# Loading the message stage's rows into two alternating sets of six buffers

## The chip, the cores and the metric

The kernel runs on one core of one Trainium2 chip. The metric is the device time of one execution in microseconds (us). A profiled execution gives the rows that are read below.

## The reference

Two graph layers run on 6250 nodes with 64 features and 206250 edges, the self loops among them, sorted by their destination. The change lies in the last step of the first layer, where each edge's message (64 features in each of 4 heads, 256 numbers) is weighted by the edge's attention and added up over the edges of a destination:

```python
alpha = segment_softmax(alpha, i, N_NODES)
msg = out_j * alpha[:, :, None]
aggr = jax.ops.segment_sum(msg, i, num_segments=N_NODES)
out = aggr.mean(1) + bias
```

`out_j` (one row of 256 numbers for an edge) was computed by earlier stages and lies in DRAM, in the two tensors `rows0` and `rows1`. A row there has 324 numbers, of which the message stage reads the first 256. The second layer is a graph convolution (`gcn_conv` twice), with a layer norm behind each layer.

## The kernel before

The kernel is a sequence of stages, each with its own tiles, and with a barrier of all engines between two of them. Only `message_stage` is touched. It goes through 152 iterations of 6 units (`BU = 6`); a unit is 256 rows, as 128 partitions by `UT = 2`. The 152 iterations are two parts of 75 and 77 (`z.its`). `paired_parts` emits each part as pairs of iterations: the first pair straight, the pairs between as a loop whose body holds two iterations, then the last pair and one single iteration straight. Of the 37 pairs of the first part 35 are in its loop, and 36 of the second part's 38, so that 142 iterations run inside the loops and 10 are straight code.

For unit j of iteration i the engines do this:

- **SP** (`load`) waits until the rows of iteration i-1 in buffer `oj[j]` are used (`oj_used[j]`) and issues the DMA `oj[j]<-rows` of 256 KB at L2330. Its queue is in order: what waits for unit 3 holds back units 4 and 5.
- **POOL** (`weigh`) first copies the iteration's attention into `heads` (L2340) and then makes the weighted message `msg[j]` (L2346) for the units of `WEIGHED`, 0, 1, 2, 4 and 5. Each waits for its DMA (`oj_in[j]`) and until TensorE has read the message of iteration i-1 (`summed[j]`).
- **DVE** makes the second one-hot matrix `onem` (L2386) of units 0, 2 and 4, weighs unit 3 itself (L2391), and adds each unit's sum from PSUM into `acc` (L2400). In front of each unit it reads the unit's block number into a register (`value_load`). Its order within an iteration is: onem of unit 2, add 0, message 3, add 1, onem 4, add 2, add 3, onem of the next iteration's unit 0, add 4, add 5.
- **ACT** makes the other one-hot matrices (L2358, L2368) and copies the attention beside the message (L2371).
- **PE** sums: two products of `onem` and `msg` into `psm[j]` (L2425), which the trace shows as 4 matmuls for a unit. It waits for `onem`, the message and the attention of its unit, in the order of the units.

The lines that set these waits are:

```python
wait(eng, oj_used[j], i)                                   # SP, before the load of unit j
eng.wait_ge(oj_in[j], (i + 1) * 16)                        # POOL, and DVE for unit 3
wait(eng, summed[j], i)                                    # POOL, before it writes msg[j]
eng.wait_ge(oj_used[j], i + 1)                             # PE, the message is there
```

The tiles and semaphores are made per unit number: 6 `oj`, 6 `msg`, 6 PSUM banks.

Of the kernel before, what the change touches and what calls it, by code (L numbers as in the profile page):

```python
# [15 lines left out]
fp32 = mybir.dt.float32  # L16
# [6 lines left out]
P = 128  # L23
D = 64
H = 4
C = H * D
K = 8
UT = 2
BU = 6
# [71 lines left out]
def wait(eng, semaphore, value):  # L101

    if not isinstance(value, int) or value > 0:
        eng.wait_ge(semaphore, value)


def rounds(eng, n, emit, start=0):

    if n - start > 0:
        emit(start)  # L110
    if n - start > 2:
        with eng.Fori(start + 1, n - 1) as i:
            emit(i)
    if n - start > 1:
        emit(n - 1)
# [12 lines left out]
def paired_parts(eng, counts, emit):  # L128

    first = 0  # L130
    for h, n in enumerate(counts):
        def two(i, first=first, h=h):
            emit(first + 2 * i, h)
            emit(first + 2 * i + 1, h)

        rounds(eng, n // 2, two)
        emit(first + n - 1, h)
        first += n


# [5 lines left out]
def seg(i, j, depth):  # L146

    return (i + 1, j - depth) if j >= depth else (i, j)
# [2146 lines left out]
def message_stage(nc, z, m, sb, ps, sem):  # L2295

    n_it = z.NU // BU
    with ExitStack() as ctx:
        oj = [sb(ctx, f"oj{j}", [P, UT, H, D], fp32) for j in range(BU)]
        ND = BU  # L2300
        msg = [sb(ctx, f"msg{q}", [P, UT, C + H], fp32) for q in range(ND)]
        one = [sb(ctx, f"onem{q}", [P, UT, P], fp32) for q in range(ND)]
        psm = [ps(ctx, f"psm{q}", [P, 512], fp32) for q in range(BU)]
        dist = [sb(ctx, f"dist_m{q}", [P, UT, P], fp32) for q in range(ND)]
        heads = sb(ctx, "heads", [P, H, BU * UT], fp32)
        heads_kept = sem(ctx, "heads_kept")
        WEIGHED, BOTH = (0, 1, 2, 4, 5), (1, 3, 5)
        second_ready = [sem(ctx, f"onem_second{j}") for j in range(BU)]
        dist_ready = sem(ctx, "distm_ready")
        placing = sem(ctx, "placing")  # L2310
        one_ready = [sem(ctx, f"onem_ready{j}") for j in range(BU)]
        oj_in, oj_used, weights_ready, summed, added = ([sem(ctx, f"{s}{j}") for j in range(BU)] for s in (
            "oj_in", "oj_used", "weights_ready", "msg_summed", "msg_added"))
        block = ctx.enter_context(nc.Block())
        rows = [r.rearrange("(u p k) c -> u p k c", p=P, k=UT) for r in m["rows"]]

        def tiles(i, j, h):

            h = int(i >= z.its[0]) if isinstance(i, int) else h
            return rows[h][span((i - h * z.its[0]) * BU + j, 1)].rearrange("o p k c -> (o p) k c")  # L2320

        def last(i):
            return isinstance(i, int) and i == n_it - 1

        @block.sync
        def _(eng):
            def load(i, h):
                for j in range(BU):
                    wait(eng, oj_used[j], i)
                    eng.dma_start(oj[j][:, :, :, :].rearrange("p k h d -> p k (h d)"),  # L2330
                                  tiles(i, j, h)[:, :, 0:C]).then_inc(oj_in[j], 16)

            paired_parts(eng, z.its, load)

        @block.gpsimd
        def _(eng):
            def weigh(i, h):
                wait(eng, oj_used[WEIGHED[-1]], i)
                eng.sem_inc(placing, 1)
                eng.tensor_copy(heads[:, :, :], m["alpha"][:, :, span(i * BU * UT, BU * UT)]).then_inc(heads_kept, 1)  # L2340
                eng.wait_ge(heads_kept, i + 1)
                for j in WEIGHED:
                    eng.wait_ge(oj_in[j], (i + 1) * 16)
                    wait(eng, summed[j], i)
                    eng.sem_inc(placing, 1)
                    eng.tensor_tensor(msg[j][:, :, 0:C].rearrange("p k (h d) -> p k h d", h=H), oj[j][:, :, :, :],  # L2346
                                      heads[:, :, j * UT:(j + 1) * UT].rearrange("p h t -> p t h")[:, :, :, None]
                                      .to_broadcast([P, UT, H, D]), ALU.mult).then_inc(oj_used[j], 1)

            paired_parts(eng, z.its, weigh)  # L2350

        @block.scalar
        def _(eng):
            def away(i, j):
                o, c = before(i, j, ND, BU)
                wait(eng, summed[o], c)
                for k in range(UT if j in BOTH else 1):
                    ins = eng.activation(dist[j % ND][:, k, :], m["io128"][:, :], ACT.Abs,  # L2358
                                         bias=m["nloA"][:, span((i * BU + j) * UT + k, 1)])
                ins.then_inc(dist_ready, 1)  # L2360

            def body(i, h):
                for j in range(BU):
                    if not (last(i) and j + 1 >= BU):
                        away(*seg(i, j + 1, BU))
                    eng.wait_ge(dist_ready, i * BU + j + 1)
                    n = UT if j in BOTH else 1
                    eng.activation(one[j % ND][:, 0:n, :], dist[j % ND][:, 0:n, :], ACT.Relu, bias=1.0,  # L2368
                                   scale=-1.0).then_inc(one_ready[j], 1)

                    eng.copy(msg[j % ND][:, :, C:C + H],  # L2371
                             m["alpha"][:, :, span((i * BU + j) * UT, UT)].rearrange("p h t -> p t h"))\
                       .then_inc(weights_ready[j], 1)

            away(0, 0)
            paired_parts(eng, z.its, body)

        @block.vector
        def _(eng):
            def product(i, j):  # L2380
                q = j % ND
                o, c = before(i, j, ND, BU)
                t = (i * BU + j) * UT
                wait(eng, summed[o], c)
                if j not in BOTH:
                    eng.tensor_scalar(one[q][:, 1, :], m["io128b"][:, :], m["nloA"][:, span(t + 1, 1)], 0.0, ALU.add,  # L2386
                                      ALU.is_equal).then_inc(second_ready[j], 1)
                if j in WEIGHED:
                    return
                eng.wait_ge(oj_in[j], (i + 1) * 16)  # L2390
                eng.tensor_tensor(msg[q][:, :, 0:C].rearrange("p k (h d) -> p k h d", h=H), oj[j][:, :, :, :],  # L2391
                                  m["alpha"][:, :, span(t, UT)].rearrange("p h t -> p t h")[:, :, :, None].to_broadcast([P, UT, H, D]),
                                  ALU.mult).then_inc(oj_used[j], 1)

            def add(i, j, b):
                eng.wait_ge(summed[j], i + 1)
                o, c = before(i, j, 1, BU)
                wait(eng, added[o], c)
                a = m["acc"][:, bass.ds(b, 1), :].rearrange("p o c -> p (o c)")
                eng.tensor_tensor(a, a, psm[j][:, 0:C + H], ALU.add).then_inc(added[j], 1)  # L2400

            def body(i, h):
                for j in range(BU):
                    b = eng.value_load(m["blkS"][0:1, 0, span(i * BU + j, 1)], min_val=0, max_val=z.HB - 1)
                    if not (last(i) and j + 2 >= BU):
                        product(*seg(i, j + 2, BU))
                    add(i, j, b)

            product(0, 0)
            product(0, 1)  # L2410
            paired_parts(eng, z.its, body)

        @block.tensor
        def _(eng):
            def sums(i, h):
                for j in range(BU):
                    q = j % ND
                    eng.wait_ge(one_ready[j], i + 1)
                    if j not in BOTH:
                        eng.wait_ge(second_ready[j], i + 1)  # L2420
                    eng.wait_ge(oj_used[j], i + 1)
                    eng.wait_ge(weights_ready[j], i + 1)
                    wait(eng, added[j], i)
                    for k in range(UT):
                        mm = eng.matmul(psm[j][:, 0:C + H], one[q][:, k, :], msg[q][:, k, :], start=(k == 0),  # L2425
                                        stop=(k == UT - 1))
                    mm.then_inc(summed[j], 1)

            paired_parts(eng, z.its, sums)
# [703 lines left out]
```

## Time and profile before

| | us |
|---|---|
| median of 3 runs | 6508.17 |
| lowest and highest of them | 6492.07, 6529.35 |
| the profiled execution, its own time | 6569.77 |
| its span | 6568.1 |
| message stage in it, first instruction to last | 4927.5 to 6036.0 |

The page shares the span out over the engines: PE is busy for 4909.4 us (75%), DVE 4742.2 (72%), ACT 4010.7 (61%) and POOL 3842.7 (59%). The message stage is slices 31 to 37 of its 40, with PE at 8 tenths in nearly all of them, ACT, POOL and DMA at 7, DVE at 6 or 7, and TensorE's granted clock at 9 tenths or more. No engine is full there, so the stage is read by waits and in order of time. In the rows, "issue" as the releaser means that the profile shows nothing that ended the idle time: register work of the sequencer, a branch, or a wait that can't be told.

### The profile page before, as it was taken

What the parts mean: (1) busy time and instruction counts of PE and PEld (TensorE: products, weight loads), DVE (VectorE), ACT (ScalarE), POOL (GpSimd) and SP (SyncE); (2) the same over time, 40 slices, a digit from 0 to 9 for tenths busy, and PEclk for the clock granted to TensorE, in tenths of its full rate; (3) what the DMA queues carried; (4) which work ended last, traced back from release to release, by engine and by line L of the source; (5) the groups of instructions that cost most, each with busy time, mean ns of one, the idle gap of its engine ahead of it and who ended that gap; (6) DMA issues with size and microseconds to landing.
All of it is one profiled execution on the core that took longest, in us unless ns stands there. A gap on an engine that the chain in (4) does not pass through costs nothing. (4 is left out here: it accounts for less than half of the span.)

```text
span 6568.1 us, 161934 instructions
## 1 busy us (share of the span) xinstructions
PE 4909.4 (75%) x32887; PEld 3154.3 (48%) x32888; DVE 4742.2 (72%) x21938; ACT 4010.7 (61%) x10577; POOL 3842.7 (59%) x5381
## 2 busy tenths in 40 slices
PE   1466676776767666674999999999948888886699
PEld 0234444444444344442555555555525556554699
DVE  6566666666666666664999999999986767777333
ACT  4344555555555555554999999989967777776100
POOL 1366666666666666565666666666637777776000
PEclk8577777777778888777999999999979999998799
DMA  8755555555555455555444444444417777775698
GB/s 227 232 180 180 188 188 182 186 185 186 189 174 179 167 172 178 168 177 153 104 103 104 103 105 105 103 103 104 103 40 218 216 216 224 215 212 176 247 360 345
DMA packets 1161941, 1148.62 MB, mean 175 GB/s; under 512 B 516532, under 2 KB 1023523, under 8 KB 1142980
## 3 DMA queue, kind: packets, MB, share of 16 engines
q1 hardware_dynamic: 1033656, 743.67, 40.2%
q0 software_dynamic: 88560, 319.28, 13.0%
q10 hardware_dynamic: 39580, 84.01, 3.4%
q8 instruction: 57, 0.93, 0.1%
q14 instruction: 88, 0.72, 0.0%
HBM read 716.98 MB, written 429.60 MB: 175 GB/s over the span
## 5 line engine op out<-in xcount | busy, mean ns | idle before, releaser
L914 POOL DMA_INDIRECT rows<-rowS,idx x1616 | 1732.5, 1072 | 1006.7 <-issue 469.7
L1185 PE MATMUL psa<-one_c,one_s 128*128 128x392 bf16 x2352 | 641.3, 393 | 654.8 <-DVE one_s L996 414.9
L2425 PE MATMUL psm<-msg,onem 128*128 128x260 f32 x3648 | 915.8, 394 | 212.7 <-issue 180.5
L988 DVE TENSOR_TENSOR one_c<-ioc,pairS 128x1176 bf16<-128x1176 f16 x784 | 599.4, 765 | 603.8 <-remote 340.4
L1699 DVE CUSTOM_DVE_ANT_1 junk<-bufh,attb 128x128 bf16<-128x128 f32 x3648 | 973.7, 301 | 0.0
L2346 POOL TENSOR_TENSOR msg<-oj,heads 128x512 f32<-128x512 f32 x760 | 796.9, 1072 | 215.3 <-DMA oj<-rows 179.0
L2425 PEld LDWEIGHTS psm<-msg,onem 128*128 128x128 f32 x3648 | 649.9, 190 | 478.2 <-issue 402.0
L1078 ACT ACTIVATE lgS<-preS 128x1024 f32<-128x1024 f32 x404 | 413.2, 1023 | 729.6 <-remote 375.4
L1659 POOL TENSOR_SCALAR one<-io128b,side 128x128 bf16<-128x128 bf16 x912 | 738.9, 810 | 63.5 <-DMA side<-rows 40.1
L1782 PE MATMUL pre<-P3h,oneT 128*128 x5472 | 757.0, 275 | 0.0
L1694 DVE CUSTOM_DVE_ANT_0 junk<-bufh,attb 128x64 bf16<-128x64 f32 x3648 | 742.1, 238 | 10.2 <-ACT bufh L1742 6.4
L1071 ACT ACTIVATE cnts<-psa 128x392 bf16<-128x392 f32 x784 | 371.7, 490 | 557.8 <-remote 209.9
L2358 ACT ACTIVATE dist_m<-io,sums_lanes 128x128 f32<-128x128 f32 x1368 | 499.1, 396 | 296.8 <-PE psm L2425 267.5
L1777 PE MATMUL pre<-W2d,eaTh 64*128 64x256 f32 x3648 | 641.9, 429 | 0.0
L1185 PEld LDWEIGHTS psa<-one_c,one_s 128*128 128x128 bf16 x2352 | 226.5, 110 | 850.8 <-DVE one_s L996 553.3
L1667 POOL COPY eaC<-side 128x128 f32<-128x128 f32 x912 | 296.1, 325 | 579.1 <-PE turned L1769 573.1
L1168 PE MATMUL preS<-W2d,eaT 64*128 64x256 f32 x3232 | 616.6, 512 | 19.7 <-ACT eaT L1089 14.1
L1738 ACT ACTIVATE lg<-pre 128x512 f32<-128x512 f32 x912 | 544.5, 597 | 137.8 <-PE pre L1782 105.0
L1782 PEld LDWEIGHTS pre<-P3h,oneT 128*128 128x128 bf16 x5472 | 460.9, 98 | 345.2 <-issue 302.9
L1742 ACT ACTIVATE bufh<-lg 128x512 f32<-128x512 f32 x912 | 574.7, 630 | 29.0
L1168 PEld LDWEIGHTS preS<-W2d,eaT 64*128 64x128 f32 x3232 | 365.1, 244 | 251.6 <-issue 197.5
L2400 DVE TENSOR_TENSOR acc<-acc,psm 128x260 f32 x912 | 380.9, 418 | 112.0 <-DVE acc L2400 66.2
(306 smaller groups left out, 9238.3 us busy)
## 6 DMA issues: line engine op xcount, KB each, us to landing
oj<-rows SPq DMA_DIRECT2D x912, 256.0 KB
bufh<-rows SPq DMA_DIRECT2D x912, 128.0 KB, 2.5
adj<-adj SPq DMA_DIRECT2D x70, 1568.0 KB, 9.9
adj<-cnts ACTq DMA_DIRECT2D x49, 1568.0 KB
side<-rows SPq DMA_DIRECT2D x912, 68.0 KB, 2.3
eaS<-in_edge_attr_dram SPq DMA_DIRECT2D x201, 256.0 KB
low<-dlow SPq DMA_DIRECT2D x202, 252.0 KB
adj_early<-adj SPq DMA_DIRECT2D x28, 1568.0 KB, 8.4
```

The lines of the kernel that those rows point to most:

```text
L914: eng.indirect_dma_start(out=m["rows"][h], out_offset=bass.IndirectOffsetOnAxis(ap=idx[s][:, k:k + 1], axis=0), in_=rows[s][:, k, :], in_o ...
L988: eng.tensor_tensor(one_c[r][:, :, :].rearrange("p k (a w) -> p k a w", w=WIDE), m["ioc"][:, q, None, :].rearrange("p k (a w) -> p k a w", ...
L1168: eng.matmul(pre[h][:, q, a * C:(a + 1) * C], eaT[j][q * D:(q + 1) * D, 2 * h + a, :], m["W2d"][q * D:(q + 1) * D, :], start=(a == 0), sto ...
L1185: mm = eng.matmul(psa[r][:, 0:z.GC], one_s[r][:, k, :], one_c[r][:, k, :], start=(k == 0), stop=(k == GT - 1))
L1659: eng.tensor_scalar(one[j % PRE][:, 1, :], m["io128b"][:, :], side[j][:, 1, LANE - C:LANE - C + 1], 0.0, ALU.add, ALU.is_equal).then_inc(s ...
L1694: ins = eng.tensor_tensor_reduce(junk[q][:, k * H + h, 0, :], buf[j][:, k, 1, h * D:(h + 1) * D], attb[:, 1, h, :], 1.0, 0.0, ALU.mult, AL ...
L1699: ins = eng.tensor_tensor_reduce(junk[q][:, k * H + h, :, :], buf[j][:, k, :, h * D:(h + 1) * D], attb[:, :, h, :], 1.0, 0.0, ALU.mult, AL ...
L1742: eng.activation(buf[j][:, :, 1, 0:C], lg[q][:, :, :], ACT.Ln, bias=1.0).then_inc(sp_ready[j], 1)
L1777: eng.matmul(pre[j % PRE][:, k, 0:C], eaT[q][k * D:(k + 1) * D, :], m["W2d"][k * D:(k + 1) * D, :], start=True, stop=False, skip_group_che ...
L1782: mm = eng.matmul(pre[j % PRE][:, k, 0:C], oneT[q][:, k * P:(k + 1) * P], P3[:, bass.ds(b, 1), n, :].rearrange("p o c -> p (o c)"), start= ...
L2346: eng.tensor_tensor(msg[j][:, :, 0:C].rearrange("p k (h d) -> p k h d", h=H), oj[j][:, :, :, :], heads[:, :, j * UT:(j + 1) * UT].rearrang ...
L2425: mm = eng.matmul(psm[j][:, 0:C + H], one[q][:, k, :], msg[q][:, k, :], start=(k == 0), stop=(k == UT - 1))
```

## The change

A second set of six buffers is added: `oj[a][j]`, where a is the parity of the iteration, with a semaphore `oj_in[a][j]` for each. `twin_parts` takes the place of `paired_parts` on SP, POOL and DVE and hands the parity a and the number of earlier turns of that set (`turn`) to the body. SP now waits for the use of iteration i-2 in place of i-1. What POOL and DVE wait for on `summed`, the six `msg` buffers and all of ACT and PE stay.

```diff
+def twin_parts(eng, counts, emit):
+
+    first = 0
+    for h, n in enumerate(counts):
+        def two(i, first=first, h=h):
+            for a in range(2):
+                emit(first + 2 * i + a, h, (first + a) % 2, (first + a) // 2 + i)
+
+        rounds(eng, n // 2, two)
+        emit(first + n - 1, h, (first + n - 1) % 2, (first + n - 1) // 2)
+        first += n
...
-        oj = [sb(ctx, f"oj{j}", [P, UT, H, D], fp32) for j in range(BU)]
+        oj = [[sb(ctx, f"oj{a}{j}", [P, UT, H, D], fp32) for j in range(BU)] for a in range(2)]
...
-            def load(i, h):
+            def load(i, h, a, turn):
                 for j in range(BU):
-                    wait(eng, oj_used[j], i)
-                    eng.dma_start(oj[j][:, :, :, :].rearrange("p k h d -> p k (h d)"),
-                                  tiles(i, j, h)[:, :, 0:C]).then_inc(oj_in[j], 16)
+                    wait(eng, oj_used[j], i - 1)
+                    eng.dma_start(oj[a][j][:, :, :, :].rearrange("p k h d -> p k (h d)"),
+                                  tiles(i, j, h)[:, :, 0:C]).then_inc(oj_in[a][j], 16)
...
-                    eng.wait_ge(oj_in[j], (i + 1) * 16)
+                    eng.wait_ge(oj_in[a][j], (turn + 1) * 16)
                     wait(eng, summed[j], i)
...
-                    if not (last(i) and j + 2 >= BU):
-                        product(*seg(i, j + 2, BU))
+                    if j + 2 < BU:
+                        product(i, j + 2, a, turn)
+                    elif not last(i):
+                        product(i + 1, j + 2 - BU, 1 - a, turn + a)
                     add(i, j, b)
```

Two places show how it stands in the instructions. The first is the start of the message stage on SP. A name behind "waits" is only the semaphore's number by the name of its first user; that there is a wait is what counts. Before:

```order
L2330 DMA oj<-rows 128x2x256 x6
L2330 DMA oj<-rows 128x2x256 [waits pairs_wide]
L2330 DMA oj<-rows 128x2x256 [waits pairs_out]
L2330 DMA oj<-rows 128x2x256 [waits ends_ready]
L2330 DMA oj<-rows 128x2x256 [waits ends_spread]
L2330 DMA oj<-rows 128x2x256 [waits low_ready]
L2330 DMA oj<-rows 128x2x256 [waits low_out]
L112 UNCONDITIONAL_BRANCH
L112 ISA
L2330 ISA [waits pairs_wide]
L2330 DMA oj<-rows 128x2x256
```

With the change:

```order
L2344 DMA oj<-rows 128x2x256 x12
L112 UNCONDITIONAL_BRANCH
L112 ISA
L2344 ISA [waits step_used0]
L2344 DMA oj<-rows 128x2x256
```

The six loads of the second iteration no longer wait; within the loop each load still has one wait.

The second place is DVE inside the loop, from the add of unit 0 (`acc`) to that of unit 1, with the message of unit 3 (`msg`) between. Before:

```order
L2400 ISA [waits exp_doneS1,copied3]
L2400 TENSOR_TENSOR acc<-acc,psm 128x260
L2404 ISA
L2404 TENSOR_LOAD blkS
L2404 ISA x2
L2390 REGISTER_ALU [waits ranked]
L2391 ISA [waits blk_ready]
L2391 TENSOR_TENSOR msg<-oj,sums_lanes 128x2x256
L2400 ISA [waits turned_ready,oh_ready]
L2400 TENSOR_TENSOR acc<-acc,psm 128x260
```

With the change:

```order
L2414 ISA [waits idx_ready,built1]
L2414 TENSOR_TENSOR acc<-acc,psm 128x260
L2418 ISA
L2418 TENSOR_LOAD blkS
L2418 ISA x2
L2405 ISA [waits adj_stored0,copied0]
L2405 TENSOR_TENSOR msg<-oj,sums_lanes 128x2x256
L2414 ISA [waits copied3,built2]
L2414 TENSOR_TENSOR acc<-acc,psm 128x260
```

No engine instruction moved on DVE; of the register work in front of message 3 one row is gone in this iteration of the loop's two.

## Rows read from the trace of the kernel before

**Rows 1.** The page: the profiled execution's span

```profile
span 6568.1 us, 161934 instructions
```

**Rows 2.** Busy time of POOL's line 2340, once an iteration, in two stretches inside the loops

```profile
4950.00:5450.00 500.00, 24.90 (x69) 1.00 0.73 216
5510.00:6000.00 490.00, 23.09 (x67) 1.00 0.72 214
```

**Rows 3.** Groups of instructions, 4940 to 6020 us (busy us, mean ns | idle before)

```profile
L2425 PE MATMUL psm<-msg,onem 128*128 128x260 f32 x3568 | 894.5, 394 | 185.5 <-issue 178.8 <-POOL msg L2346 1.0 <-DVE onem L2386 0.9
L2346 POOL TENSOR_TENSOR msg<-oj,heads 128x512 f32<-128x512 f32 x746 | 782.0, 1072 | 208.7 <-DMA oj<-rows 172.9 <-POOL heads L2340 35.3
...
L2386 DVE TENSOR_SCALAR onem<-io128b,sums_lanes 128x128 f32<-128x128 bf16 x446 | 308.5, 692 | 176.3 <-issue 171.4
...
L2391 DVE TENSOR_TENSOR msg<-oj,sums_lanes 128x512 f32<-128x512 f32 x149 | 135.4, 908 | 33.8 <-issue 32.9
L2340 POOL COPY heads<-sums_lanes 128x48 f32 (+1 forms) x149 | 52.1, 349 | 38.8 <-POOL msg L2346 38.8
```

**Rows 4.** Waits, 4940 to 6020 us: us in total, times, longest

```profile
POOL msg L2346 <- DMA oj<-rows: 172.9, 168, 1.9
...
DVE acc L2400 <- PE psm L2425: 37.4, 71, 0.6
```

**Rows 5.** Waits of the SP queue, 4940 to 6020 us

```profile
SPq L2330 <- DVE msg L2391: 392.6, 149, 3.5
```

**Rows 6.** Timeline of DVE: start us, us, then the idle time before

```profile
5210.76 1.02 DVE L2386 TENSOR_SCALAR onem<-io128b,sums_lanes 128x128 f32<-128x128 bf16 x1 [0.91 <-issue]
...
5212.04 0.69 DVE L2391 TENSOR_TENSOR msg<-oj,sums_lanes 128x512 f32<-128x512 f32 x1
...
5213.21 0.52 DVE L2386 TENSOR_SCALAR onem<-io128b,sums_lanes 128x128 f32<-128x128 bf16 x1
...
5214.46 0.43 DVE L2400 TENSOR_TENSOR acc<-acc,psm 128x260 f32 x1 [0.40 <-DVE acc L2400]
5215.36 0.41 DVE L2386 TENSOR_SCALAR onem<-io128b,sums_lanes 128x128 f32<-128x128 bf16 x1 [0.47 <-issue]
...
5216.52 0.43 DVE L2400 TENSOR_TENSOR acc<-acc,psm 128x260 f32 x1 [0.42 <-DVE acc L2400]
5217.40 0.75 DVE L2386 TENSOR_SCALAR onem<-io128b,sums_lanes 128x128 f32<-128x128 bf16 x1 [0.46 <-issue]
...
5222.02 1.18 DVE L2386 TENSOR_SCALAR onem<-io128b,sums_lanes 128x128 f32<-128x128 bf16 x1 [0.47 <-issue]
...
5223.77 0.42 DVE L2400 TENSOR_TENSOR acc<-acc,psm 128x260 f32 x1 [0.24 <-DVE acc L2400]
5225.11 1.07 DVE L2386 TENSOR_SCALAR onem<-io128b,sums_lanes 128x128 f32<-128x128 bf16 x1 [0.91 <-issue]
```

**Rows 7.** Timeline of POOL, the same stretch

```profile
5209.62 2.08 POOL L2346 TENSOR_TENSOR msg<-oj,heads 128x512 f32<-128x512 f32 x2 [0.87 <-DMA oj<-rows]
5211.96 0.22 POOL L2340 COPY heads<-sums_lanes 128x48 f32 x1 [0.26 <-POOL msg L2346]
...
5217.02 2.07 POOL L2346 TENSOR_TENSOR msg<-oj,heads 128x512 f32<-128x512 f32 x2 [1.34 <-DMA oj<-rows]
```

**Rows 8.** Timeline of PE, the same stretch

```profile
5211.88 5.98 PE L2425 MATMUL psm<-msg,onem 128*128 128x260 f32 x24 [0.96 <-issue]
```

**Rows 9.** Timeline of DVE, an iteration with short waits for the port

```profile
5489.16 0.43 DVE L2386 TENSOR_SCALAR onem<-io128b,sums_lanes 128x128 f32<-128x128 bf16 x1 [0.61 <-issue]
...
5490.43 0.69 DVE L2391 TENSOR_TENSOR msg<-oj,sums_lanes 128x512 f32<-128x512 f32 x1 [0.50 <-issue]
...
5491.54 0.58 DVE L2386 TENSOR_SCALAR onem<-io128b,sums_lanes 128x128 f32<-128x128 bf16 x1
...
5495.65 0.46 DVE L2386 TENSOR_SCALAR onem<-io128b,sums_lanes 128x128 f32<-128x128 bf16 x1 [0.46 <-issue]
```

**Rows 10.** One tile: onem on DVE, ns min/median/max

```profile
L2386 DVE TENSOR_SCALAR onem<-io128b,sums_lanes x446: 270/574/1190, 4940.8 to 6018.8; 128x128 f32<-128x128 bf16 x149
```

More of the change, by code:

```diff
@@ L2311, in message_stage @@
         one_ready = [sem(ctx, f"onem_ready{j}") for j in range(BU)]
-        oj_in, oj_used, weights_ready, summed, added = ([sem(ctx, f"{s}{j}") for j in range(BU)] for s in (
-            "oj_in", "oj_used", "weights_ready", "msg_summed", "msg_added"))
+        oj_used, weights_ready, summed, added = ([sem(ctx, f"{s}{j}") for j in range(BU)] for s in (
+            "oj_used", "weights_ready", "msg_summed", "msg_added"))
+        oj_in = [[sem(ctx, f"oj_in{a}{j}") for j in range(BU)] for a in range(2)]
         block = ctx.enter_context(nc.Block())
@@ L2326, in _, with weigh @@
         def _(eng):
-            def load(i, h):
+            def load(i, h, a, turn):
                 for j in range(BU):
-                    wait(eng, oj_used[j], i)
-                    eng.dma_start(oj[j][:, :, :, :].rearrange("p k h d -> p k (h d)"),
-                                  tiles(i, j, h)[:, :, 0:C]).then_inc(oj_in[j], 16)
-            paired_parts(eng, z.its, load)
+                    wait(eng, oj_used[j], i - 1)
+                    eng.dma_start(oj[a][j][:, :, :, :].rearrange("p k h d -> p k (h d)"),
+                                  tiles(i, j, h)[:, :, 0:C]).then_inc(oj_in[a][j], 16)
+            twin_parts(eng, z.its, load)
         @block.gpsimd
         def _(eng):
-            def weigh(i, h):
+            def weigh(i, h, a, turn):
                 wait(eng, oj_used[WEIGHED[-1]], i)
@@ L2342, in weigh @@
                 for j in WEIGHED:
-                    eng.wait_ge(oj_in[j], (i + 1) * 16)
+                    eng.wait_ge(oj_in[a][j], (turn + 1) * 16)
                     wait(eng, summed[j], i)
                     eng.sem_inc(placing, 1)
-                    eng.tensor_tensor(msg[j][:, :, 0:C].rearrange("p k (h d) -> p k h d", h=H), oj[j][:, :, :, :],
+                    eng.tensor_tensor(msg[j][:, :, 0:C].rearrange("p k (h d) -> p k h d", h=H), oj[a][j][:, :, :, :],
                                       heads[:, :, j * UT:(j + 1) * UT].rearrange("p h t -> p t h")[:, :, :, None]
                                       .to_broadcast([P, UT, H, D]), ALU.mult).then_inc(oj_used[j], 1)
-            paired_parts(eng, z.its, weigh)
+            twin_parts(eng, z.its, weigh)
         @block.scalar
@@ L2379, in _, with product @@
         def _(eng):
-            def product(i, j):
+            def product(i, j, a, turn):
                 q = j % ND
@@ L2389, in product @@
                     return
-                eng.wait_ge(oj_in[j], (i + 1) * 16)
-                eng.tensor_tensor(msg[q][:, :, 0:C].rearrange("p k (h d) -> p k h d", h=H), oj[j][:, :, :, :],
+                eng.wait_ge(oj_in[a][j], (turn + 1) * 16)
+                eng.tensor_tensor(msg[q][:, :, 0:C].rearrange("p k (h d) -> p k h d", h=H), oj[a][j][:, :, :, :],
                                   m["alpha"][:, :, span(t, UT)].rearrange("p h t -> p t h")[:, :, :, None].to_broadcast([P, UT, H, D]),
@@ L2400, in add, with body @@
                 eng.tensor_tensor(a, a, psm[j][:, 0:C + H], ALU.add).then_inc(added[j], 1)
-            def body(i, h):
+            def body(i, h, a, turn):
                 for j in range(BU):
                     b = eng.value_load(m["blkS"][0:1, 0, span(i * BU + j, 1)], min_val=0, max_val=z.HB - 1)
-                    if not (last(i) and j + 2 >= BU):
-                        product(*seg(i, j + 2, BU))
+                    if j + 2 < BU:
+                        product(i, j + 2, a, turn)
+                    elif not last(i):
+                        product(i + 1, j + 2 - BU, 1 - a, turn + a)
                     add(i, j, b)
-            product(0, 0)
-            product(0, 1)
-            paired_parts(eng, z.its, body)
+            product(0, 0, 0, 0)
+            product(0, 1, 0, 0)
+            twin_parts(eng, z.its, body)
         @block.tensor
```

## The prediction

> **What bounds the kernel now.** The change touches only the message stage, 1108 us of the profiled span [rows 1], so I read that stage first by groups, then by waits, then in order of time.
>
> Inside the loops an iteration takes (500 + 490) / (69 + 67) = 7.28 us, counted by POOL's once-an-iteration copy [rows 2]. The groups rule out that an engine is full: in 1080 us PE is idle for 185.5, and POOL is busy for 782.0 + 52.1 [rows 3]. POOL waits 172.9 us for the rows' DMA over 149 iterations, 1.16 us each [rows 3, 4], and SP waits 392.6 us for DVE's message of unit 3 [rows 5]. That is the wait which the change takes away: the load of unit 4 stands in SP's queue behind unit 3's, which waits for DVE. What is it worth? PE waits for a message of POOL for only 1.0 us in those 1080, and for "issue" 178.8 [rows 3]. So POOL's late start is not what holds PE.
>
> Order of time shows what does. From unit 2's onem at 5210.76 to add 5 at 5216.52 the idle time before DVE's instructions is ended by "issue" (register reads, a branch) or by DVE's own last add, never by PE or POOL [rows 6]. Waits of its adds for PE are 37.4 us in all, 0.25 an iteration [rows 4]. The shared port: an onem takes 270 ns at least and 692 on average [rows 10, 3]. The one at 5210.76 took 1.02 us and ended at 5211.78, 0.08 after POOL's instructions that ended at 5209.62 + 2.08 = 5211.70 [rows 6, 7]. **DVE's chain sets the pace, and POOL matters to it by when it holds the port.**
>
> The Trainium skill's page "SBUF — State Buffer", section "Who interferes with whom", says this as a rule: VectorE in a two-port mode and GpSimd take a shared pair exclusively for a whole instruction, and whoever issued first makes the other block. The trace agrees, with the 0.08 us above.
>
> **DVE's steps, start to start,** with d the duration of the first instruction of a step:
> - onem 0 to add 5: 1.16 (5215.36 to 5216.52, d 0.41), but d + 0.57 when onem is long (5222.02 to 5223.77 is 1.75, d 1.18), since add 4 and then add 5 follow it one after the other. So d costs beyond 0.59 [rows 6].
> - add 5 to onem 2: 0.88 (to 5217.40), and 1.34 across the loop's branch, once in two iterations (5223.77 to 5225.11) [rows 6].
> - onem 2 to message 3: 1.28 with d 1.02 (5210.76 to 5212.04), so d + 0.26 [rows 6]; 1.27 with d 0.43, which is the register read's floor [rows 9]. A long onem 2 is nearly free.
> - message 3 to onem 4: 1.11 with d 0.69 [rows 9], taken as d + 0.26 when longer.
> - onem 4 to add 3: 1.25 with d 0.52 (5213.21 to 5214.46), d + 0.57 when longer. Add 3 to onem 0: 0.90 (to 5215.36) [rows 6].
>
> A quiet iteration takes 6.49 us (5489.16 to 5495.65, onem 2 to onem 2) [rows 9]; half a branch more (0.46 / 2) makes 6.72. The loops' 7.28 hold 0.56 us of port waits and waits for PE.
>
> **The change, part by part.**
> - *Loads one iteration earlier.* POOL's DMA wait goes, 1.16 us an iteration, off the critical path. SP has room: its queue waits 392.6 of 1080 us [rows 5].
> - *What is late next on POOL.* It may run ahead only until `summed` of the previous iteration. Unit 4's message started at 5217.02 [rows 7], and PE had finished unit 4 of the iteration before at about 5211.88 + 3 x 1.0 = 5214.9 (six units in 5.98 us from unit 2 on) [rows 8]. There are 2.1 us to gain, and POOL needs 5 x 1.07 + 0.35 for its work [rows 3] and 0.26 + 0.28 around the copy [rows 7], 6.24 in all, under 7.28. So POOL advances until it waits for PE at unit 4.
> - *Where this puts POOL's instructions.* Let onem 4 end at E. PE starts unit 4 at E + 0.10 (onem ended at 5211.78, PE started at 5211.88) [rows 6, 8], takes about 1.1, and POOL follows some 0.15 later: at E + 1.35. The 0.15 is an estimate from the 0.10 between DVE and PE; 0.1 or 0.3 would do. DVE meanwhile runs add 2 (from E - 0.08) and add 3 (E + 0.57) and wants the port for onem 0 at E + 1.46. POOL has just taken it. That holds in each iteration, since both count from E.
> - *The walk.* Set onem 0's start to 0. It waits for POOL's unit 4, which ends at 0.95, and has d 1.03. Add 5 at 1.60. POOL: unit 5 to 2.0, copy, unit 0 from 2.85 to 3.9. Without the branch: onem 2 at 2.48 finds the port free; message 3 at 3.75 is behind unit 0 until 3.9 and ends near 4.45; unit 1 takes the port until 5.45; onem 4 at 4.86 ends at 5.53, d 0.67; add 3 at 6.11; onem 0 at 7.0. With the branch: onem 2 at 2.94 waits for unit 0 to 3.98, d 1.04; message 3 at 4.24 waits for unit 1 to 4.92, d 1.23; onem 4 at 5.73 waits for unit 2, d 0.8; add 3 at 7.1; onem 0 at 8.0. The mean is 7.5 against 7.28: **+0.22 us an iteration**, over 142 loop iterations +31 us.
> - *Straight iterations.* Ten, where a DMA wait can hurt since DVE does less register work. Bounds 0 and 10 x 1.16 = 12 us; I take 4, as a third of the waits on the path would make: -4.
> - *At nothing:* six buffers more in memory, six semaphores, twelve loads at the start instead of six (POOL needs the first ones, which come as before), one register row less on DVE. POOL's and SP's extra register work hides in their slack of 1.0 us and more.
>
> **Sum:** +31 - 4 = +27 us on the profiled execution's 6569.8, as on the median 6508.2: 6535. The profiled execution is 1% over that median, so I carry the difference over, not the level. The walk rests on offsets of 0.1 us, so its unknowns are wide: port waits could go altogether, which bounds the gain at 0.56 x 142 = 79 us plus 12, or onem 0 could be passed over at the border of two POOL instructions and wait through part of both. The one at 5222.02 took 1.18 us, more than one such instruction (1.07) [rows 6, 3]; 1.05 more is the bound.
>
> **Rivals.**
> - *The wait was worth something (14%).* With POOL ahead, its work falls where DVE wants no port. Half the port waits gone: -0.28 x 142 - 4 = -44, 6464; all: 6425. For it: the quiet iteration of 6.49 exists. Against: it needs POOL to stay out of step with PE, while `summed` ties it in step. The Trainium skill's page "Trainium Kernel Development and Optimization", section "Best Practices", asks to double-buffer so that DMA and compute overlap. By it the 1.16 us would come back. Here they already overlap.
> - *Nothing (28%).* Port waits are as long as before at other places: -4 to +10 us, 6511. For it: POOL is as busy as before in the same time, and DVE asks as often, so chance alone would give the same mean.
> - *The walk holds (38%):* +10 to +45 us, 6535.
> - *A convoy (20%), the case on the other side, clearly slower.* POOL runs units 4 and 5 back to back, and onem 0 asks near their border. If it loses the border it waits 1.05 us more. It decides once more than one iteration in three does so: 142 / 3 x 1.05 = +50 on top, 6584; one in six gives 6558.
> - That the change doesn't do what it says (the loads stay late) would be "nothing" again: SP issued at most six loads in 7.28 us before and has to do no more.
>
> **How the numbers follow.** A measurement of this kernel can tell about 0.5%, 32 us. Faster: 14%. Same: 28% and half of the walk's case, 48%. Slower: its other half and the convoy, 38%. The range leaves out half of the first case and half of the last: 6465 to 6580.
>
> **What would show it.** In the changed profile POOL's wait for the DMA is gone and a wait for PE's `psm` of some 0.3 to 1 us an iteration stands there, at unit 4. Onem 0 takes 0.9 to 1.1 us nearly always, where it now varies between 0.41 and 1.18. The period is 7.4 to 7.6. I am wrong if onem's mean falls below 0.6 us with a period under 7.1 (the first rival), or if PE starts to wait for POOL by name, which would mean that POOL's place on the path was missed.

## The result, and the profile after

The change made the kernel slower: 6561.77 us median (6538.71 to 6568.88, 5 runs) against 6508.17, a ratio of 1.0074 with a 95% interval of 1.0051 to 1.0097, or 48 us by that ratio. The profiled execution's span is 6567.2 us, as long as before's [rows 1]; the two profiles differ in other stages by as much, so the message stage is read by itself. It runs from 4884.7 to 6036.1 us, 1151.4 us, where it took 1108.5 (the table of the kernel before). Those 42.9 us agree with the result, whose interval is 33 to 63 us.

The period comes from POOL's copy, once an iteration. To compare the two loops, each window here holds exactly 64 iterations. The columns are the window, its length, POOL's busy time (count), the granted clock, the DMA share and GB/s. Before:

```profile
4971.40:5436.80 465.40, 23.16 (x64) 1.00 0.73 216
5519.40:5989.20 469.80, 21.92 (x64) 1.00 0.72 214
```

After:

```profile
4929.00:5400.50 471.50, 14.25 (x64) 1.00 0.72 213
5483.50:5986.50 503.00, 14.26 (x64) 1.00 0.68 200
```

Before, both loops run at nearly the same period, 7.27 and 7.34 us. After, the first loop takes 471.5 / 64 = 7.37 and the second 503.0 / 64 = 7.86. The loops hold the same work, and before the change their periods were 0.07 us apart; now it is 0.49. That is the first thing to explain.

The groups of instructions after, in both loops and the straight code between (busy us, mean ns | idle before), to be read against [rows 3]:

```profile
L2360 POOL TENSOR_TENSOR msg<-oj,heads 128x512 f32<-128x512 f32 x700 | 760.1, 1107 | 229.5 <-issue 191.5 <-POOL heads L2354 37.9
...
L2400 DVE TENSOR_SCALAR onem<-io128b,sums_lanes 128x128 f32<-128x128 bf16 x420 | 328.1, 781 | 163.0 <-issue 160.2
...
L2405 DVE TENSOR_TENSOR msg<-oj,sums_lanes 128x512 f32<-128x512 f32 x140 | 152.0, 1086 | 42.8 <-issue 38.2
```

The DMA is gone from POOL's releasers, where it had 172.9 us. SP's wait for DVE's message 3, which the prediction called the wait that the change takes away, is still there (442.3 us from 4900 to 6020 us, against 392.6 in [rows 5]). SP still runs ahead until this wait stops it, only one iteration further, so its size did not say that the loads were late. POOL still idles for 229.5 us, more than before. Its own instructions grew from 1072 to 1107 ns, DVE's `onem` from 692 to 781 and DVE's message of unit 3 from 908 to 1086. The waits, against [rows 4]:

```profile
PE psm L2441 <- issue: 230.2, 356, 1.5
POOL msg L2360 <- issue: 201.4, 212, 1.5
```

PE waits for "issue" longer than before (230.2 against 178.8 us in [rows 3], in a window 4% longer). The view names nobody for it; the order of time below does.

In order of time, DVE in two iterations of the first loop (start us, us, idle time before it):

```profile
5133.12 1.06 DVE L2400 TENSOR_SCALAR onem<-io128b,sums_lanes 128x128 f32<-128x128 bf16 x1 [0.47 <-issue]
...
5135.64 0.29 DVE L2400 TENSOR_SCALAR onem<-io128b,sums_lanes 128x128 f32<-128x128 bf16 x1 [0.46 <-issue]
...
5136.87 0.69 DVE L2405 TENSOR_TENSOR msg<-oj,sums_lanes 128x512 f32<-128x512 f32 x1 [0.53 <-issue]
...
5140.02 1.07 DVE L2400 TENSOR_SCALAR onem<-io128b,sums_lanes 128x128 f32<-128x128 bf16 x1 [0.46 <-issue]
...
5147.85 1.06 DVE L2400 TENSOR_SCALAR onem<-io128b,sums_lanes 128x128 f32<-128x128 bf16 x1 [0.47 <-issue]
```

POOL in the first of them:

```profile
5133.04 2.08 POOL L2360 TENSOR_TENSOR msg<-oj,heads 128x512 f32<-128x512 f32 x2 [1.47 <-issue]
...
5135.90 3.60 POOL L2360 TENSOR_TENSOR msg<-oj,heads 128x512 f32<-128x512 f32 x3 [0.29 <-POOL heads L2354]
5139.95 2.07 POOL L2360 TENSOR_TENSOR msg<-oj,heads 128x512 f32<-128x512 f32 x2 [0.45 <-issue]
```

and PE:

```profile
5137.67 2.99 PE L2441 MATMUL psm<-msg,onem 128*128 128x260 f32 x12 [0.52 <-issue]
```

PE's twelve matmuls are units 3, 4 and 5. They start at 5137.67, 0.11 us behind the end of DVE's message 3 (5136.87 + 0.69 = 5137.56), so it is still DVE that PE waits for. Unit 4 ends near 5137.67 + 2.1 = 5139.8, and POOL's next message of unit 4 starts at 5139.95. DVE's onem of unit 0 ("onem 0") starts at 5140.02, 0.07 us behind it, and takes 1.07 us. The same stands at 5133.12 (after 5133.04), and at 5147.85. Onem 0 does not vary as in [rows 6]: in all 128 iterations of the two windows it takes 1.06 to 1.08 us. The iteration without the branch takes 5140.02 - 5133.12 = 6.90 us, the other 5147.85 - 5140.02 = 7.83.

In the second loop the iteration without the branch goes another way. DVE, then POOL:

```profile
5568.16 1.07 DVE L2400 TENSOR_SCALAR onem<-io128b,sums_lanes 128x128 f32<-128x128 bf16 x1 [0.46 <-issue]
...
5570.70 0.28 DVE L2400 TENSOR_SCALAR onem<-io128b,sums_lanes 128x128 f32<-128x128 bf16 x1 [0.47 <-issue]
...
5571.97 1.59 DVE L2405 TENSOR_TENSOR msg<-oj,sums_lanes 128x512 f32<-128x512 f32 x1 [0.56 <-issue]
...
5576.03 1.06 DVE L2400 TENSOR_SCALAR onem<-io128b,sums_lanes 128x128 f32<-128x128 bf16 x1 [0.47 <-issue]
```

```profile
5570.94 3.54 POOL L2360 TENSOR_TENSOR msg<-oj,heads 128x512 f32<-128x512 f32 x3 [0.29 <-POOL heads L2354]
```

Message 3 takes 1.59 us here and 0.69 in the first loop. What differs is who comes first, message 3 or POOL's message of unit 1, the second of the three. That one by itself, in the first loop and in the second:

```profile
5136.91 1.57 POOL L2360 TENSOR_TENSOR msg<-oj,heads 128x512 f32<-128x512 f32 x1
...
5571.96 1.06 POOL L2360 TENSOR_TENSOR msg<-oj,heads 128x512 f32<-128x512 f32 x1
```

In the first loop message 3 starts 0.04 us ahead of it (5136.87) and takes 0.69 us, and POOL's instruction is the long one, 1.57 us. In the second, message 3 starts 0.01 us behind it (5571.97) and is itself the long one. The whole trace bears this out, at the resolution of its time stamps. In the 32 such iterations of the first loop's window message 3 is ahead by 23 to 52 ns, and short each time. In the second loop's window it is level or up to 20 ns behind in 30 of 32, and long each time; in the other two it is 1 ns ahead, and short. The long iteration takes 5576.03 - 5568.16 = 7.87 us.

### The profile page after: what moved, and what is told of

It is laid out like the page before. It is cut to its first block and busy times, and to the rows that moved or that the text cites. A ratio compares the mean times of both kernels' runs of the same rounds, so it can differ in the third digit from the quotient of the medians.

```text
span 6567.2 us, 161899 instructions
## 1 busy us (share of the span) xinstructions
PE 4865.4 (74%) x32887; PEld 3127.9 (48%) x32888; DVE 4806.9 (73%) x21938; ACT 4010.3 (61%) x10577; POOL 3851.3 (59%) x5381
## 5 line engine op out<-in xcount | busy, mean ns | idle before, releaser
L927 POOL DMA_INDIRECT rows<-rowS,idx x1616 | 1731.8, 1072 | 964.3 <-issue 468.3
L1198 PE MATMUL psa<-one_c,one_s 128*128 128x392 bf16 x2352 | 626.3, 384 | 664.4 <-DVE one_s L1009 414.3
L2360 POOL TENSOR_TENSOR msg<-oj,heads 128x512 f32<-128x512 f32 x760 | 825.0, 1107 | 248.4 <-issue 203.3
L1181 PE MATMUL preS<-W2d,eaT 64*128 64x256 f32 x3232 | 603.4, 504 | 25.1 <-issue 13.0
L2400 DVE TENSOR_SCALAR onem<-io128b,sums_lanes 128x128 f32<-128x128 bf16 x456 | 353.1, 774 | 181.8 <-issue 171.3
```

Of the source, the lines that this page charges most:

```text
L927: eng.indirect_dma_start(out=m["rows"][h], out_offset=bass.IndirectOffsetOnAxis(ap=idx[s][:, k:k + 1], axis=0), in_=rows[s][:, k, :], in_o ...
L1181: eng.matmul(pre[h][:, q, a * C:(a + 1) * C], eaT[j][q * D:(q + 1) * D, 2 * h + a, :], m["W2d"][q * D:(q + 1) * D, :], start=(a == 0), sto ...
L1198: mm = eng.matmul(psa[r][:, 0:z.GC], one_s[r][:, k, :], one_c[r][:, k, :], start=(k == 0), stop=(k == GT - 1))
```

## The experiments

Ratios are to runs of the kernel before on the same chip, with a 95% interval. The chips differ in level (the kernel before took 6170, 6174 and 6567 us in the three groups of runs), so only ratios are compared. P is the theory of the prediction: the loss is DVE's waiting for the shared port, and the change only moved POOL's instructions onto DVE's. The kernels e0, e1, e5 and e4 ran together on one chip, then e2, e3, e6 and e8 on a second, then e9 and e10 on a third.

**e0_after_again: the changed kernel once more.** No edit.

> The changed kernel once more, for a second profile and times beside the other runs. Theory P (port): 1.007 of before again, and in the loops the same fixed cycle: tile 0's onem on DVE takes 1.06 to 1.07 us in every iteration because POOL took the port for unit 4 just before. Theory N (chance, the profile of one run only): other durations in a second profile. It also tells whether the two loops keep their different periods (7.37 us in the first, 7.89 in the second).

1.0081 (1.0061 to 1.0101).

The same 64 iterations took 471.5 us in the first loop and 502.8 in the second, while the whole kernel took 6220 us here and 6562 in the result. Onem 0 takes 1.06 to 1.08 us in all 128 again. The cycle and the difference between the loops belong to the program, not to chance.

**e1_late_loads: all of the change but the early loads.**

```diff
-                    wait(eng, oj_used[j], i - 1)
+                    wait(eng, oj_used[j], i)
```

> Twelve buffers, semaphores and the new index arithmetic as in the changed kernel, but SP waits for the use of iteration i-1, as before the change, so the loads come no earlier. Theory P: POOL is late again through the DMA, its place against DVE is as before, and the time is that of before (0.998 to 1.002). Rival M (the cost is the memory, the semaphores or the register work): as the changed kernel, 1.007.

0.9997 (0.9986 to 1.0009). Period and groups, both loops:

```profile
4573.10:5039.10 466.00, 23.84 (x64) 1.00 0.73 216
5121.60:5587.60 466.00, 22.55 (x64) 1.00 0.74 216
```

```profile
L2360 POOL TENSOR_TENSOR msg<-oj,heads 128x512 f32<-128x512 f32 x700 | 734.8, 1072 | 192.5 <-DMA oj<-rows 161.3 <-POOL heads L2354 30.0
...
L2400 DVE TENSOR_SCALAR onem<-io128b,sums_lanes 128x128 f32<-128x128 bf16 x420 | 289.4, 689 | 165.5 <-issue 160.7
```

Memory, semaphores and register work cost nothing, so rival M falls. POOL waits for the DMA again and onem is back at 689 ns. The cost comes with the early loads: through them, or through when POOL works. The next run tells these two apart.

**e5_msg_twelve: the early loads, without the tie to PE.** The message buffers are doubled too; ACT's distance tiles go from six to three to make room.

```diff
-                    wait(eng, summed[j], i)
+                    wait(eng, summed[j], i - 1)
...
-                    eng.tensor_tensor(msg[j][:, :, 0:C].rearrange("p k (h d) -> p k h d", h=H), oj[a][j][:, :, :, :],
+                    eng.tensor_tensor(msg[a][j][:, :, 0:C].rearrange("p k (h d) -> p k h d", h=H), oj[a][j][:, :, :, :],
```

> The changed kernel with twelve message buffers as well, so that POOL is no longer held by PE's sums of the iteration before (three distance tiles on ACT instead of six, to make room). POOL then runs ahead until the loads hold it again, which wait for DVE's message of unit 3 two iterations before, so at the same place of DVE's iteration as in the kernel before. Theory P: time of before, 0.997 to 1.003, and onem's mean back near 0.69 us. Rival L (loads further ahead cost by themselves: more transfers in flight): 1.007 or more.

0.9995 (0.9983 to 1.0007). Groups, both loops:

```profile
L2360 POOL TENSOR_TENSOR msg<-oj,heads 128x512 f32<-128x512 f32 x700 | 740.2, 1081 | 180.2 <-DMA oj<-rows 146.8 <-POOL heads L2354 32.1
...
L2402 DVE TENSOR_SCALAR onem<-io128b,sums_lanes 128x128 f32<-128x128 bf16 x419 | 277.3, 662 | 164.3 <-issue 159.4
```

SP waits for the same as in the changed kernel, so the loads may run as far ahead, and they cost nothing: rival L falls. POOL may be an iteration further ahead, waits for the DMA again, and onem is at 662 ns. What the changed kernel's POOL waited for was PE: the view called it "issue", but it vanishes with `summed` one iteration back. The loops run at 7.18 and 7.20 us, a little under e1's 7.28, which the kernel's time does not show clearly.

**e4_hold_unit4: a wait more, and faster.**

```diff
                 for j in WEIGHED:
+                    if j == 4:
+                        eng.wait_ge(second_ready[0], i + 1)
                     eng.wait_ge(oj_in[a][j], (turn + 1) * 16)
```

> The changed kernel with one wait more: POOL takes unit 4's message only after DVE's onem of tile 0 of the same iteration. Theory P: that onem finds the port free (0.3 to 0.6 us instead of 1.07), a walk through both kinds of iteration gives 6.6 and 7.5 us, mean 7.05 against 7.6 in the changed kernel and 7.28 before: 0.993 to 0.997 of before, faster than both. Rivals M and L: as the changed kernel or slower, since only a wait is added.

0.995 (0.9933 to 0.9967), faster than both kernels. DVE in an iteration of each kind, then POOL:

```profile
4766.23 0.29 DVE L2402 TENSOR_SCALAR onem<-io128b,sums_lanes 128x128 f32<-128x128 bf16 x1 [0.47 <-issue]
...
4772.65 0.57 DVE L2402 TENSOR_SCALAR onem<-io128b,sums_lanes 128x128 f32<-128x128 bf16 x1 [0.46 <-issue]
...
4776.42 1.38 DVE L2407 TENSOR_TENSOR msg<-oj,sums_lanes 128x512 f32<-128x512 f32 x1 [0.50 <-issue]
...
4780.29 0.29 DVE L2402 TENSOR_SCALAR onem<-io128b,sums_lanes 128x128 f32<-128x128 bf16 x1 [0.47 <-issue]
```

```profile
4766.72 2.07 POOL L2362 TENSOR_TENSOR msg<-oj,heads 128x512 f32<-128x512 f32 x2 [1.04 <-DVE onem L2402]
...
4776.20 3.54 POOL L2362 TENSOR_TENSOR msg<-oj,heads 128x512 f32<-128x512 f32 x3 [0.20 <-POOL heads L2354]
```

Onem 0 takes 0.29 us where POOL's unit 4 (4766.72) now starts behind it (4766.23). It takes 0.57 in the other iteration, where POOL is still at unit 2 until 4773.14. The iterations take 6.42 and 7.64 us, near the walked 6.6 and 7.5. What is left is at 4776.42: message 3 takes 1.38 us, because POOL's unit 0 had started at 4776.20.

**e2_onem_psum_twelve and e3_onem_psum_six: onem without the port.** In both, DVE's onem reads its counting row from a PSUM tile that is filled once. The row is fp32 there, where it was bf16 before, so two things change at once.

```diff
-                    eng.tensor_scalar(one[q][:, 1, :], m["io128b"][:, :], m["nloA"][:, span(t + 1, 1)], 0.0, ALU.add,
+                    eng.tensor_scalar(one[q][:, 1, :], psio[:, 0:P], m["nloA"][:, span(t + 1, 1)], 0.0, ALU.add,
```

> The changed kernel (twelve buffers), but DVE's onem reads its counting row from PSUM instead of from memory, so that it should not need the port it shares with POOL. Message 3 still needs it. Theory P: onem takes about 0.3 us everywhere with no wait, the period falls from 7.6 to 6.8 to 7.1 us and the time to 0.988 to 0.994 of before. Rival Q (DVE's long onem has another cause than POOL): onem stays at 0.7 us and more, time 1.007.

> The same edit on the kernel before (six buffers). Theory P: with the onem's port waits gone the two kernels come together: 0.988 to 0.994 here too, within 0.3% of e2_onem_psum_twelve, and what is left is message 3's wait. Rival W (the early loads have a worth of their own once DVE is quicker): the twelve-buffer version is faster than this one by over 0.3%.

e2 1.0023 (1.0011 to 1.0035), a miss; e3 0.9935 (0.992 to 0.995), as expected by itself, but not within 0.3% of e2. The groups of e2:

```profile
L2407 DVE TENSOR_TENSOR msg<-oj,sums_lanes 128x512 f32<-128x512 f32 x140 | 177.4, 1267 | 75.9 <-issue 75.9
...
L2402 DVE TENSOR_SCALAR onem<-psio,sums_lanes 128x128 f32<-128x128 f32 x420 | 145.8, 347 | 155.7 <-issue 155.6
```

and of e3:

```profile
L2393 DVE TENSOR_TENSOR msg<-oj,sums_lanes 128x512 f32<-128x512 f32 x140 | 152.6, 1090 | 75.4 <-issue 75.4
L2388 DVE TENSOR_SCALAR onem<-psio,sums_lanes 128x128 f32<-128x128 f32 x419 | 145.8, 348 | 157.4 <-issue 156.1
```

Onem takes 347 ns in both, its wait is gone, and rival Q falls. Whether it is the PSUM tile or the fp32 row that does it, no run tells. The two kernels did not come together. With twelve buffers all the collisions went to message 3, the one instruction that still needs the port: 1267 ns against 1090. The second cause shows in the granted clock, in e2 only. A window before one such place and one in it:

```profile
4720.00:4729.00 9.00, 6.45 (x28) 4.56 (x27) 5.90 (x12) 6.55 (x27) 8.20 (x9) 1.00 0.74 220
4729.00:4732.40 3.40, 3.40 (x8) 2.64 (x9) 1.54 (x5) 0.99 (x4) 0.71 (x1) 0.50 0.58 162
```

and PE there:

```profile
4728.89 7.22 PE L2445 MATMUL psm<-msg,onem 128*128 128x260 f32 x24 [1.31 <-issue]
```

PE had been idle for 1.31 us, then its clock was granted at 0.50, the 1.2 GHz level, for 3.4 us: 8 matmuls in 3.4 us, where [rows 8] have 24 in 5.98, some 13 or 14 in 3.4. The clock's record has 18 such stretches in e2's message stage and at most one in any other run. Of the 128 iterations in e2's two loops, counted from onem 0 to onem 0, 34 touch one; the other 94 take 7.21 us on average, all of them 7.42. So the clock goes with some 0.2 x 142 = 30 us of e2's time, 0.5%. By this estimate e2 would be near 0.998 without it, still short of what was expected.

**e6_hold_units_4_0: one hold too many.** e4, with unit 0 held until message 3 of the iteration before is done (`wait(eng, oj_used[3], i)` for j == 0).

> e4_hold_unit4 with one wait more: POOL takes unit 0's message only after DVE's message of unit 3 of the iteration before. In e4 the iterations with the branch still lost 1.65 - 1.10 us there (message 3 took 1.39 us). Theory P, walked: those iterations go from 7.64 to about 7.1 us, the others stay at 6.45, so 0.26 us an iteration, 37 us: 0.988 to 0.991 of before. If holding POOL back makes it late for PE, the time rises over e4's 0.995.

0.998 (0.9967 to 0.9992): a miss, slower than e4. DVE, then POOL:

```profile
4774.12 0.69 DVE L2409 TENSOR_TENSOR msg<-oj,sums_lanes 128x512 f32<-128x512 f32 x1
...
4775.23 1.08 DVE L2404 TENSOR_SCALAR onem<-io128b,sums_lanes 128x128 f32<-128x128 bf16 x1
```

```profile
4775.17 3.09 POOL L2364 TENSOR_TENSOR msg<-oj,heads 128x512 f32<-128x512 f32 x3 [1.01 <-DVE msg L2409]
```

Message 3 takes 0.69 us, as wanted. But it releases POOL, which starts unit 0 at 4775.17, and DVE's onem 4 at 4775.23 comes 0.06 us too late: 1.08 us. The collision moved to the next step of the same chain, in the iterations without the branch too, which the expectation had left at 6.45 us: the loops run at 7.09 and 7.25.

**e8_onem_psum_hold0: nothing left to meet.** The changed kernel with e2's onem and e6's hold of unit 0, without the hold of unit 4.

> e2_onem_psum_twelve with unit 0's message held until DVE's message 3 is done, so that no instruction of DVE meets POOL on the port. Theory P: the period falls to DVE's floor, 6.5 us and 6.95 with the branch, mean 6.72: 0.56 x 142 = 79 us under before, 0.986 to 0.989, the fastest of all. POOL needs 6.24 us an iteration, so if it becomes the bound the period is 6.8 to 6.9 instead.

0.9863 (0.9845 to 0.9882), the fastest kernel here. Periods and groups:

```profile
4587.60:5017.60 430.00, 14.26 (x64) 1.00 0.79 234
5094.10:5525.10 431.00, 14.25 (x64) 1.00 0.79 234
```

```profile
L2364 POOL TENSOR_TENSOR msg<-oj,heads 128x512 f32<-128x512 f32 x700 | 717.2, 1058 | 147.3 <-DVE msg L2409 145.6 <-POOL heads L2356 1.7
...
L2404 DVE TENSOR_SCALAR onem<-psio,sums_lanes 128x128 f32<-128x128 f32 x420 | 147.3, 351 | 164.3 <-issue 155.9
L2409 DVE TENSOR_TENSOR msg<-oj,sums_lanes 128x512 f32<-128x512 f32 x140 | 100.4, 717 | 75.8 <-issue 75.8
```

430.0 / 64 = 6.72 and 431.0 / 64 = 6.73 us. That is the floor of 6.72 that the prediction had worked out from the quiet iteration [rows 9] and half a branch. Message 3 takes 717 ns, onem 351. With the port waits gone, the 0.56 us above the floor of the kernel before are gone too; that they were port waits and what hung on them is the reading that fits, and no run takes them apart further.

**e9_onem_psum_hold0_six: the same with six buffers.**

> e8_onem_psum_hold0 without the second set: six buffers, onem's row from PSUM, unit 0 held until message 3. It asks what the twelve buffers are worth once POOL keeps out of DVE's way. Theory P: with six buffers the DMA still sets POOL's units 4 and 5, unit 5 lies on message 3 as in e3 (message 3 took 1.0 to 1.2 us), and the held unit 0 came later anyway; so the time is e3's, 0.992 to 0.995, and twelve buffers are worth 0.6 to 0.8% here. Rival H (the hold alone does it, buffers are worth nothing): 0.986 to 0.988, as e8.

0.9962 (0.9944 to 0.9979): POOL and message 3 in its groups:

```profile
L2350 POOL TENSOR_TENSOR msg<-oj,heads 128x512 f32<-128x512 f32 x700 | 737.6, 1079 | 160.8 <-DMA oj<-rows 130.6 <-POOL heads L2342 28.5
...
L2395 DVE TENSOR_TENSOR msg<-oj,sums_lanes 128x512 f32<-128x512 f32 x141 | 153.3, 1087 | 76.0 <-issue 76.0
```

Rival H falls: message 3 takes 1087 ns, as in e3, since the DMA (130.6 us of POOL's idle time) still sets when POOL comes. The ratio is a little worse than expected, with intervals of e3 and e9 that meet. Twelve buffers, useless to harmful by themselves, are worth about 1% here (e8 against e9, which differ in nothing else but ran on different chips).

**e10_hold_unit1: the border in the second loop.** The changed kernel, with POOL's unit 1 held until message 3.

> The changed kernel with one wait more: POOL takes unit 1's message only after DVE's message 3 of the iteration before. In the changed kernel the branchless iterations took 6.91 us in the first loop and 7.82 in the second; message 3 asked for the port 0.04 us before POOL's unit 1 there and 0.01 us after it here. Theory P (that border is the whole difference): both loops come to the same period, message 3 takes 0.69 us in both; walked, 7.15 and 7.64 us, mean 7.4 against 7.37 and 7.86, so the time is 1.002 to 1.005 of before. Rival S (something else in the second loop is slower): the loops stay apart by over 0.3 us.

1.0053 (1.0034 to 1.0071). Both loops, then POOL and message 3:

```profile
4959.70:5439.40 479.70, 14.25 (x64) 1.00 0.71 210
5522.70:6006.50 483.80, 14.26 (x64) 1.00 0.70 208
```

```profile
L2407 DVE TENSOR_TENSOR msg<-oj,sums_lanes 128x512 f32<-128x512 f32 x140 | 97.8, 698 | 42.5 <-issue 38.1
```

7.50 and 7.56 us: the loops came together, message 3 takes 698 ns, and rival S falls. The half microsecond between the loops of the changed kernel was that one border. The periods are 0.10 and 0.16 us above the walk's 7.4, and the ratio is just above the expected 1.002 to 1.005.

## Why the prediction was right, and where it was off

- **What bounds the stage: right.** DVE's chain sets the pace and POOL's wait for the DMA is off it. In e5 the early loads by themselves are worth nothing, e4 gets faster although POOL waits for more, and e8, with the port waits gone, has the floor of 6.72 us. Only SP's wait was misread: it is not what the change took away, as said above.
- **What is late next on POOL: right.** It waits for PE at unit 4 and starts 0.17 us or so behind PE's end, where 0.15 was taken. The wait was larger, up to 1.47 us where 0.3 to 1 was said. The profile named it "issue" and not PE, against what the prediction had looked for; e5 settled it.
- **Onem 0 behind POOL's unit 4, each time: right.** 1.06 to 1.08 us in every iteration of both loops, predicted 1.03. e4 takes it away, and the loops go from 7.37 and 7.86 to 7.03 and 7.09 us, though message 3's waits change with it.
- **The walk's size: two errors that partly cancel.** It gave 7.0 and 8.0 us, 7.5 on average. Where its order of events held, in the first loop, it gave too much: 6.90 and 7.83, or 7.37, only 0.10 us above before's 7.27. At that rate the change would have cost 0.10 x 142 = 14 us, close to the case "nothing". In the second loop one step failed, the iteration without the branch, where "message 3 ... ends near 4.45" (0.7 us). It took 1.59, and the iteration 7.87 instead of 7.0. The walk had message 3 at 3.75, counted from onem 0's start, and POOL's unit 1 at 3.9, behind unit 0. Unit 1 came at 3.79 and 3.80 in the two loops (the walk took 0.35 us for POOL's copy in front of them, and it takes 0.22), and message 3 at 3.75 in the first and 3.81 in the second. So of the 0.15 us there were 0.04 left in one loop and nothing in the other. Why message 3 comes 0.06 us later in the second loop stays open.
- **The sum over the loops.** The increase is (7.37 + 7.86) / 2 - (7.27 + 7.34) / 2 = 0.31 us and 44 us, not 0.22 and 31. The second loop has 0.52 us of it and the first 0.10, so some five sixths of the loss come from the loop in which message 3 waits out POOL's unit 1. This is the kind of event that the convoy rival described, DVE passed over at the border between two POOL instructions, at message 3 instead of onem 0.
- **The straight iterations:** -4 was taken. 42.9 us for the stage less 44 for the loops leaves -1.
- **The sum:** 6535, in place of 6562; the range of 6465 to 6580 held. That the kernel gets somewhat slower, and through onem 0, was foreseen. That the total lies so near the forecast is in part luck, since the largest share came from an event that the walk did not have. The single call was no change (0.48 against 0.38 for slower), and the measurement says slower: 0.74%, above the bound of 0.5% under which the size had been put. Two small slips: half of the walk's 38% makes 0.47 and 0.39 in these two, and the convoy at one in six gives 6560, not 6558.
- **The first rival** (POOL ahead, its work in DVE's gaps) is what e8 reaches, 1.4% under before, with two more edits. In the changed kernel `summed` puts POOL in step with PE and so with DVE, as the prediction held against this rival; without that tie e5 is no faster than before either.
- The Trainium skill's rule of "SBUF — State Buffer", section "Who interferes with whom", is that whoever issued first holds the pair for the whole instruction. The trace agrees for onem 0: in the changed kernel POOL is 0.07 us ahead and DVE waits out the instruction. Message 3 and POOL's unit 1 do the same to each other, by who is ahead. The advice of "Trainium Kernel Development and Optimization", section "Best Practices", in the Trainium skill, is to double-buffer for overlap. It cost 0.74% in the changed kernel and was worth 1% in e8 against e9.

## What to carry to other kernels

A wait that nobody on the critical path waits for can still do good: it may be what keeps two engines apart on something they share. Before deepening a buffer, ask what the freed engine will wait for next, and where in the slow engine's iteration that puts its work. If both count from the same event, the collision comes every time and not at random; then order the two by a semaphore, and check the step behind it too, where the collision may go next.

## What the hardware showed that was not expected

- The order of two starts, a few ns apart, decides about 0.9 us. In the changed kernel's two loops message 3 was short (0.69 us) in each of the 34 iterations in which it started at least 1 ns ahead of POOL's unit 1, and long (1.58 to 1.61 us) in each of the 30 in which it started with it or up to 20 ns behind. In the second profile (e0) two of the 32 in the second loop are short again, and they lie within 2 ns of level. So 64 iterations take 503.0 us instead of 471.5, alike in both profiles.
- With DMA landings as the releaser the collisions are spread: onem takes 270 to 1190 ns in [rows 10], and message 3 varies from iteration to iteration in e1, e5, e3 and e9 as well. Where POOL is released by semaphores alone they settle in a cycle: in e4, e6, e8 and e10 each of the pair's two iterations keeps its length to 0.05 us throughout a loop.
- In e2 TensorE's clock fell to the 1.2 GHz level for 3.4 us at a time, at or within 0.6 us behind the end of a gap of 1.3 us on PE, though PE was busy for over 80% of that stage. PE had 69 gaps over 1.2 us in e2's stage and the clock fell 18 times. In the changed kernel it had 37 of them and the clock fell once, 1.7 us behind the end of one. What picks the gaps out stays open.
